# Differential attention with a mixture of experts on one core: VectorE's order within a slot, and denominators in two parts

## The reference

```
s1, s2  = q @ k1.T / sqrt(8), q @ k2.T / sqrt(8)        # causal
attn    = softmax(s1) - sigmoid(lambda_logit) * softmax(s2)
attn    = attn / max(sum(|attn|), 1e-6)
x       = layernorm(x + (attn @ v) @ Wo.T)
xn      = layernorm(x) * gamma + beta
gates   = the two largest of softmax(xn @ router_w.T / 1.5), others 0
x       = layernorm(x + x + sum over e of gates[e] * (silu(xn @ W1[e]) @ W2[e]))
```

## Time and profile before

| | |
|---|---|
| median of 3 runs | 1231.5 us (1228.81 to 1231.53) |
| the profiled execution's own time | 1223.18 us |
| its span | 1221.3 us |
| granted TensorE clock, mean over the span | 0.952 of full speed |
| PE / DVE / ACT / POOL busy | 90% / 86% / 75% / 68% |
| idle of ACT ahead of `exps` until `neg_max` (L723) | 80.8 us |
| idle of DVE ahead of `neg_max` until the scores (L855) | 69.3 us |

### The profile page before, as it was taken

How to read it: one execution, slowest core, us unless ns; L and a number is a source line. 1 busy time by engine, 2 the same in 40 slices (tenths; PEclk the granted TensorE clock), 3 DMA queues, 4 the chain that set the end, 5 groups by cost and what they waited for, 6 DMA issues and landing times.

```text
span 1221.3 us, 29361 instructions
## 1 busy us (share of the span) xinstructions
PE 1103.2 (90%) x8786; PEld 725.7 (59%) x8786; DVE 1044.4 (86%) x2722; ACT 915.2 (75%) x2882; POOL 834.0 (68%) x1245
## 2 busy tenths in 40 slices
PE   3788869999899989999899997999899998999897
PEld 1355536666556655666556665666556665566565
DVE  1688788988999899999999899999999999898664
ACT  1688868888688877888688876888678886787232
POOL 2599976776768757877667776777677777677100
PEclk8577779999999999999999999999999999999899
DMA  7503400232005200142003300052002410000000
GB/s 213 126 14 80 99 1 3 62 82 48 1 14 118 70 2 2 36 110 57 1 14 86 89 15 1 21 125 57 1 2 57 89 48 1 19 1 2 1 10 9
DMA packets 62142, 54.66 MB, mean 45 GB/s; under 512 B 6050, under 2 KB 59938, under 8 KB 61986
## 3 DMA queue, kind: packets, MB, share of 16 engines
q1 hardware_dynamic: 61986, 52.78, 17.8%
HBM read 37.03 MB, written 15.73 MB: 43 GB/s over the span
## 4 chain that ended last, share of the span: by engine, by line
PE 66%; DVE 18%; issue 7%; POOL 4%; ACT 2%; SPq 1%; DMA 1%; DVEq 0%; POOLq 0%; ACTq 0%
PE side L809 14%; PE side L803 13%; PE trans L883 12%; PE scores L853 8%; PE heads L872 7%; DVE neg_max L723 6%; PE scores L855 4%; DVE abs_sum L734 3%; PE scores L803 2%; PE scores L809 2%; POOL exps L445 2%; PE side L773 2%; DVE hT L686 1%; DVE xh L566 1%; POOL exps L441 1%
## 5 line engine op out<-in xcount | busy, mean ns | idle before, releaser
L491 ACT ACTIVATE exps<-scores,neg_max 128x256 f32<-128x256 f32 (+3 forms) x1024 | 537.9, 529 | 97.5 <-DVE neg_max L723 80.8
L723 DVE TENSOR_REDUCE neg_max<-scores 128x1 f32<-128x256 f32 (+3 forms) x1024 | 448.7, 479 | 72.8 <-PE scores L855 69.3
L445 POOL TENSOR_TENSOR exps<-exps 128x384 f32<-128x384 f32 (+3 forms) x512 | 444.7, 868 | 42.7
L441 POOL TENSOR_SCALAR exps<-exps,inv_l,lam_l 128x384 f32<-128x384 f32 (+3 forms) x512 | 313.6, 613 | 141.2 <-DVE inv_l L714 138.4
L853 PE MATMUL scores<-stack 72*128 72x256 bf16 (+3 forms) x1024 | 274.1, 314 | 17.5 <-DMA stack<-parts_dram 13.5
L809 PE MATMUL side<-w_sb,hT 128*128 128x128 f32 x1816 | 253.6, 283 | 29.5 <-DVE acc L698 18.1
L883 PE MATMUL trans<-ident,exps 128*128 128x128 f32 x1280 | 254.9, 300 | 22.8 <-ACT diffT L499 19.4
L499 ACT ACTIVATE diffT<-trans 128x384 f32<-128x384 f32 (+3 forms) x512 | 223.4, 436 | 52.9 <-PE trans L883 52.1
L809 PEld LDWEIGHTS side<-w_sb,hT 128*128 128x128 f32 x1816 | 222.6, 192 | 63.7 <-DVE acc L698 29.9
L803 PE MATMUL side<-xnT,w_sb 128*128 128x512 f32 x458 | 247.2, 621 | 1.8 <-ACT xnT L526 1.0
L883 PEld LDWEIGHTS trans<-ident,exps 128*128 128x128 f32 x1280 | 150.4, 147 | 134.7 <-issue 102.5
(11 more groups left out here) (94 smaller groups left out, 685.2 us busy)
## 6 DMA issues: line engine op xcount, KB each, us to landing
stack<-parts_dram SPq DMA_DIRECT2D x288, 96.0 KB
parts_dram<-parts SPq DMA_DIRECT2D x104, 128.0 KB, 2.4
x_in<-x_dram SPq DMA_DIRECT2D x8, 256.0 KB, 4.5
w_sb<-w_dram SPq DMA_DIRECT2D x1, 2048.0 KB, 9.1
x_res<-x_dram SPq DMA_DIRECT2D x8, 256.0 KB, 4.5
o_dram<-y_out SPq DMA_DIRECT2D x8, 256.0 KB, 3.4
wq_sb<-wqT_dram SPq DMA_DIRECT2D x1, 64.0 KB
wq_sb<-wk1T_dram SPq DMA_DIRECT2D x1, 64.0 KB
```

The costliest lines, as they stand in the source:

```text
L441: nc.gpsimd.tensor_scalar(diff[:, q % 2, j, 0:w], exps[:, q % 2, 1, j, 0:w], inv_l2[:, q % 2, j:j + 1], lam_l1[:, q % 2, j:j + 1], ALU.mul ...
L445: nc.gpsimd.tensor_tensor(diff[:, q % 2, j, 0:w], diff[:, q % 2, j, 0:w], exps[:, q % 2, 0, j, 0:w], ALU.subtract).then_inc(diff_done.sem, 1)
L491: nc.scalar.activation(exps[:, q % 2, k, j, 0:w], scores[:, u % 2, k, 0:w], ACT.Exp, bias=neg_max[:, q % 2, j, k:k + 1], accum_out=sums[:, ...
L723: nc.vector.tensor_reduce(neg_max[:, q % 2, j, k:k + 1], scores[:, u % 2, k, 0:w], AX.X, ALU.max, negate=True).then_inc(max_done.sem, 1)
```

## The change

VectorE's slot begins with the two maxima of the slot's unit; what stood ahead of them (route place 0, `guard`, the side tasks, `inv_l2`, route place 1) now stands behind them. `guard` and `inv_den` are made for 32 units at once, two times a batch (slots 40 and 8) in place of once a quad, 16 times. For this `sums` and `abs_sum` get a place for every unit of a batch. No other engine's order changes.

```
+DEN_PARTS = 2
+DEN_G = NG // DEN_PARTS
+DEN_UNITS = UNITS // DEN_PARTS
...
-        sums = sb("sums", [P, 4, 2, QUAD])
+        sums = sb("sums", [P, 2, NG, NT, QUAD])
...
-        abs_sum = sb("abs_sum", [P, 2, QUAD])
-        guard = sb("guard", [P, QUAD])
+        abs_sum = sb("abs_sum", [P, NG, NT, QUAD])
+        guard = sb("guard", [P, DEN_G, NT, QUAD])
...
-        den_done = signal("den_done", 2 * QUADS)
+        den_done = signal("den_done", 2 * DEN_PARTS)
...
                 for slot in range(UNITS):
+                    for n, u in units(b, stages, slot, 0):
+
+                        q, j = divmod(u, QUAD)
+                        w = (tile_of(q) + 1) * P
+                        dve.wait_ge(exp_done.sem, exp_done.after(n, 2 * (u + 1 - 2 * QUAD)))
+                        for k in range(2):
+                            dve.wait_ge(score_done.sem, score_done.after(n, 2 * u + k + 1))
+                            nc.vector.tensor_reduce(neg_max[:, q % 2, j, k:k + 1], scores[:, u % 2, k, 0:w], AX.X,
+                                                    ALU.max, negate=True).then_inc(max_done.sem, 1)
                     route(b, stages, slot, 0)
                     for n, u in units(b, stages, slot, LAG_DEN):
-                        q, j = divmod(u, QUAD)
-                        if j == QUAD - 1:
-
-                            dve.wait_ge(abs_done.sem, abs_done.after(n, 2 * (q + 1)))
-                            nc.vector.scalar_tensor_tensor(out=guard[:, :], in0=sums[:, q % 4, 0, :], scalar=DENOM_MIN,
-                                                           in1=abs_sum[:, q % 2, :], op0=ALU.mult, op1=ALU.max)\
-                                .then_inc(den_done.sem, 1)
+                        i, last_of_part = divmod(u + 1, DEN_UNITS)
+                        if last_of_part == 0:
+
+                            part = slice((i - 1) * DEN_G, i * DEN_G)
+                            dve.wait_ge(abs_done.sem, abs_done.after(n, (u + 1) // 2))
+                            nc.vector.scalar_tensor_tensor(out=guard[:, :, :, :], in0=sums[:, 0, part, :, :],
+                                                           scalar=DENOM_MIN, in1=abs_sum[:, part, :, :],
+                                                           op0=ALU.mult, op1=ALU.max).then_inc(den_done.sem, 1)
...
-                            dve.wait_ge(den_done.sem, den_done.after(n, 2 * QUADS))
+                            dve.wait_ge(den_done.sem, den_done.after(n, 2 * DEN_PARTS))
...
                     route(b, stages, slot, 1)
-                    for n, u in units(b, stages, slot, 0):
...
                     route(b, stages, slot, 2)
                     route(b, stages, slot, 3)
...
                     for n, u in units(b, stages, slot, LAG_DEN):
-                        q, j = divmod(u, QUAD)
-                        if j == QUAD - 1:
-                            dve.wait_ge(den_done.sem, den_done.after(n, 2 * q + 1))
-                            nc.vector.reciprocal(inv_den[:, tile_of(q), q // NT:NH:NG], guard[:, :])\
-                                .then_inc(den_done.sem, 1)
+                        i, last_of_part = divmod(u + 1, DEN_UNITS)
+                        if last_of_part == 0:
+                            dve.wait_ge(den_done.sem, den_done.after(n, 2 * i - 1))
+                            nc.vector.reciprocal(
+                                inv_den[:, :, :].rearrange("p t (j g) -> p g t j", g=NG)[:, (i - 1) * DEN_G:i * DEN_G, :, :],
+                                guard[:, :, :, :]).then_inc(den_done.sem, 1)
```

More of the change, by code:

```diff
@@ L436, in body @@
                             pool.wait_ge(exp_done.sem, exp_done.after(n, 2 * (u + QUAD)))
-                            nc.gpsimd.tensor_tensor(lam_l1[:, q % 2, :], sums[:, q % 4, 0, :], lam_all[:, q // NT:NH:NG],
+                            nc.gpsimd.tensor_tensor(lam_l1[:, q % 2, :], sums[:, 0, q // NT, tile_of(q), :], lam_all[:, q // NT:NH:NG],
                                                     ALU.mult).then_inc(lam_l1_done.sem, 1)
@@ L492, in body @@
                                                  ACT.Exp, bias=neg_max[:, q % 2, j, k:k + 1],
-                                                 accum_out=sums[:, q % 4, k, j:j + 1]).then_inc(exp_done.sem, 1)
+                                                 accum_out=sums[:, k, q // NT, tile_of(q), j:j + 1]).then_inc(exp_done.sem, 1)
                         for n, u in units(b, stages, slot, LAG_COPY) if k == 0 else ():
@@ L713, in body @@
                         dve.wait_ge(diff_done.sem, diff_done.after(n, u - QUAD))
-                        nc.vector.reciprocal(inv_l2[:, q % 2, :], sums[:, q % 4, 1, :]).then_inc(inv_l2_done.sem, 1)
+                        nc.vector.reciprocal(inv_l2[:, q % 2, :], sums[:, 1, q // NT, tile_of(q), :]).then_inc(inv_l2_done.sem, 1)
                     route(b, stages, slot, 1)
-                    for n, u in units(b, stages, slot, 0):
-                        q, j = divmod(u, QUAD)
[L719 to L724, removed]
                     route(b, stages, slot, 2)
@@ L733, in body @@
                         dve.wait_ge(diff_done.sem, diff_done.after(n, u + 1))
-                        nc.vector.tensor_reduce(abs_sum[:, q % 2, j - 1:j + 1], diff[:, q % 2, j - 1:j + 1, 0:w], AX.X,
+                        nc.vector.tensor_reduce(abs_sum[:, q // NT, tile_of(q), j - 1:j + 1], diff[:, q % 2, j - 1:j + 1, 0:w], AX.X,
                                                 ALU.add, apply_absolute_value=True).then_inc(abs_done.sem, 1)
                     for n, u in units(b, stages, slot, LAG_DEN):
-                        q, j = divmod(u, QUAD)
-                        if j == QUAD - 1:
-                            dve.wait_ge(den_done.sem, den_done.after(n, 2 * q + 1))
-                            nc.vector.reciprocal(inv_den[:, tile_of(q), q // NT:NH:NG], guard[:, :])\
-                                .then_inc(den_done.sem, 1)
+                        i, last_of_part = divmod(u + 1, DEN_UNITS)
[4 more added lines that the diff above has]
+                                guard[:, :, :, :]).then_inc(den_done.sem, 1)
                     if slot == LAG_PV and "attention" in stages:
```

## The result

The changed kernel takes 1492.4 us (median of 4 runs, 1488.3 to 1494.1), the kernel before 1230.4 beside it: ratio 1.2125, 95% interval 1.2096 to 1.2155. The direction was forecast, the size was not: 1345 was named, with 1385 as the upper end of the range.

The account below looks back on a forecast made before the run. The prediction took TensorE to bound the kernel, idle only 8.6 of 142.6 us a batch. It summed 1223.2 + 153 (waits) - 28 (absorbed) = 1348, named 1345, own range 1315 to 1385, 8 in 10 within 1265 to 1385.

Parts of the forecast that it names:

- listed single places: Slots with one side task whose bank reader would now run behind the maxima, making TensorE wait; 18.5 us a batch.
- the series of the prediction: At tight places scores, two maxima, reader, side task run in series; TensorE waits 1.30 to 1.95 (hT), 0.96 to 1.61 (acc).
- ScalarE's shorter wait: ScalarE waits 80.8 us for the maxima; getting them earlier was claimed to be worth nothing.
- signs that the prediction named: Slot 2's order, VectorE busy down about 62, its scores wait up like TensorE's waits (well over 100), batch some 160 us.
- 153 - 28: Added TensorE waits over all bodies, 153 us, less 28 us taken as absorbed by TensorE's present idle time.
- 28 us of absorption: Half of TensorE's present idle time between batches, taken as given back because VectorE would less often be late.
- TensorE's idle 57 us: TensorE's present idle time, 8.6 us a batch over 6.6 batches, claimed to be partly VectorE being late.
- the count of task distances: Tight places found from two side banks used in turn: a task needs the reader of the one before the last.
- Second tasks: Second side tasks in slots with two, partly covered by the first one's 0.93 of TensorE work; 4.6 us a batch.
- VectorE as the limit: Rival: VectorE bounds the kernel and sheds 62 us, so it gets faster, 1161 or likelier 1192; chance 10%.
- Most absorbed: Rival: places cost as priced, but all 57 us idle and half the freed VectorE time come off, 1288; chance 22%.
- the two halves cancel: Rival: the maxima's order costs just what the fewer guards give, 1230; chance 4%.

Follow-up runs that it names:

- Experiment three: Denominators twice a batch as changed, maxima first only in slots 2, 34 and 50, old order elsewhere; 1252.4 us, ratio 1.0187 to the kernel before.
- loose_first: The changed kernel, but 23 tight slots keep side tasks ahead of the maxima; the other 41 have maxima first; 1248.1 us, ratio 1.0152.
- fill: The changed kernel with TensorE issuing matmuls of zeros ahead of the waits in slots 9, 10 and 17 to 22; 1431.7 us, ratio 1.1581.
- loose34: Maxima first in 34 slots: the 41 without a tight place, less slots 9, 24, 26, 28, 31, 60 and 61; 1233.4 us, ratio 0.9986.
- den_only: The kernel before with only guard and reciprocal made twice a batch, maxima where they were; 1225.7 us, ratio 0.9958.

## Why the prediction fell short

**Right.** The mechanism and, at the listed single places but slot 22, its price. TensorE's wait at the side task in one batch of the changed kernel (its start less that of the last scores matmul plus 0.06), against the series of the prediction:

| slot | reader, width | predicted | measured |
|---|---|---|---|
| 2, 34, 50 | hT, 256 | 1.50 | 1.49, 1.50, 1.50 |
| 37 | hT, 128 | 1.30 | 1.29 |
| 10 | hT, 384 | 1.73 | 1.71 |
| 14, 30, 44 | hT, 512 | 1.95 | 1.93, 1.93, 1.93 |
| 18, 20, 43 | acc, 256, 128, 384 | 1.16, 0.96, 1.39 | 1.11, 0.95, 1.38 |
| 0 | hT, 256 | 1.50 | 1.54 |
| 22 | logits, 128 | 1.0 | 2.22 |

Slot 14 has 1.93 in this batch and 1.76 in four others. Right too: guards and reciprocals shorter by 62 us in all (63), the other half of the change neither cause nor cure, ScalarE's shorter wait worth nothing, and the order scores, maxima, `hT`, side on the timeline. Of the signs that the prediction named, three came out at another size: VectorE's busy time fell by 43 and not 62, its wait for scores rose by 337 and not by about what TensorE lost, and the period of a batch is 181 and not some 160.

**Wrong, in order of size.** From the denominators alone the loss is (1.2125 - 0.9958) x 1230 = 267 us; the prediction had 153 - 28 = 125.

1. *The clock was priced at nothing.* This is the step that failed. The prediction said: "Further up lies only a lower granted clock when TensorE pauses; it was 0.99 over the batch shown". It gave that no term in its sum. That clock was the one without the pauses. Filling them in eight slots gives back 61 us net (67 by the ratios). Slots 17 to 22 have a wait almost every time, and after them TensorE's instructions take twice as long while the work behind them is late already. By the trace 123 us of busy time were added; not all lie in the way, and not all pauses were filled, so 61 to 67 is a lower bound for the clock. The slots, below, give some 80.
2. *28 us of absorption, of which some 10 existed.* The prediction took half of TensorE's idle 57 us as given back. Slot by slot, 16 and 26 shrank, by 0.67 and 0.54, and 15, 28 and 32 by 0.3 together: 10 us over 6.6 batches. Experiment three has pauses alone, and there 28 of 30 us arrive.
3. *Places that the count of task distances left out*, 24 us by loose_first; in the changed kernel slots 9, 25, 27, 61 and 62 grew by 3.0 a batch. I asked only which bank the next task waits for. `den_T` waits for `spread` in slot 9. In slots 24 to 28 VectorE stands behind a long `finish` (1.11), and in the 512-wide quads behind itself, so that readers with a slot of room came late too. The prediction named the latter and gave it 7 us.
4. *Second tasks and slot 22*: 4.6 us a batch predicted; at full clock these slots grew by 5.9, some 9 us over all. The largest misses are 13 (1.5, priced 0.7) and 49 (0.8, priced 0.2). Slot 22 grew by 2.3, priced 1.0, 8 us over all: the moments of `norm3`, a late task that falls into the same slot, stand ahead of the reads of the logits. The timeline of VectorE there:

```profile
737.12 0.49 DVE L627 TENSOR_REDUCE neg_max<-scores 128x1 f32<-128x128 f32 x2 [4.41 <-PE scores L860]
737.53 0.86 DVE L557 BATCH_NORM_STATS2 stats<-acc 128x6 f32<-128x128 f32 x4
...
738.76 0.16 DVE L684 TENSOR_REDUCE route_max<-side 128x4 f32<-128x32 f32 x1
738.95 0.19 DVE L687 TENSOR_TENSOR route_in<-side,route_max 128x32 f32<-128x32 f32 x1
```

These terms come from different runs and overlap, so they are not added up. A sum can be read from the lengths of the slots on TensorE (from a slot's first scores matmul to the next slot's), which at full clock mostly repeat from batch to batch to within 0.02. A full batch took 140.4 before and 180.9 after, the mean of bodies 2 to 6, so 40.5 more:

| us a batch | priced | measured |
|---|---|---|
| single tasks, slot 22 among them | 18.5 | 19.5 |
| second tasks | 4.6 | 5.9 |
| places left out | 0 | 3.0 |
| slots that shrank | -4.2 (28 / 6.6) | -1.5 |
| waits, together | 18.9 | 26.8 |
| lower clock | 0 | 13.6 |

The line of the waits takes each slot at full clock, and the clock has what is left. In slots 17 to 23 full clock is found in fill alone, whose zeros may lengthen a wait, so the clock may have a little more than 13.6. Over the six full bodies this is some 161 us of waits and 82 of clock. Bodies 0 and 1 lost another 28, which can't be split so, for their clock was low before the change too. The sum, 271, meets the growth of the span, 269. Shown by an experiment of their own are the clock (fill), that lone pauses arrive nearly whole (three), and the left-out places (loose34); the split by slots is a reading of traces.

The rivals: VectorE as the limit is out, since it lost 63 us of work for a gain of 5. Most absorbed is out, with 1.5 of 8.6 us a batch given back, and so is that the two halves cancel. The chances were on the right side, but the range was built from waits only, and a clock that answers to waits has no place in such a range.

## What to carry to other kernels

An in-order engine that serves two partners should do first what is ready, not what is newest: the maxima can't start before scores of their own slot, so placing them first only puts the ready readers behind a wait. Before moving a step ahead of others, list for each of the others who waits for it in the same slot, by banks, by data and by the length of what stands before it. And where TensorE is 90% busy, price a new pause twice: once as waiting, and once as the work behind it at half the clock if several pauses stand close.

## What the runs showed of the chip

- Lone pauses of 1.5 us, three a batch, left the granted clock as it was (0.948 and 0.944 in the profiled executions), while the waits in nine of the slots from 9 to 23 brought it down several times a batch, for up to 15 us at 0.50. The dip in slot 10 followed two pauses, of 1.4 us in slot 9 and 1.6 in slot 10. Matmuls of zeros in these waits brought the clock back to 0.99 over the batch.
- The guard's price is a wait for GpSimd, paid by the instruction and not by the element. Of the 128 guards before, 72 took over 200 ns, and every one of them ended within 25 ns of the end of the GpSimd instruction that was running when it started; the other 56 took 145 to 192. The guard of the earlier trace rows (696.88 + 0.73 = 697.61) ends with this one (697.60):

```profile
696.60 1.00 POOL L445 TENSOR_TENSOR exps<-exps 128x384 f32<-128x384 f32 x1
```

With 32 elements a guard took 178 to 184 where it did not wait and ended 38 to 49 ns behind the GpSimd instruction where it did. Its mean is a matter of where it falls: 355 in the changed kernel and 452 with the old order (den_only), 412 with 4 elements. The Trainium skill (SBUF — State Buffer, section Who interferes with whom) states that a VectorE instruction with two SBUF inputs contends with a GpSimd instruction that reads SBUF; the trace agrees. The reciprocal, which has one input, went from 170 to 343.
